# Layer norm and projection over eight pieces, Ln and Exp in place of square root and reciprocal, skip terms begun in the convolution, and the stored weights waited for later

## The reference, cut to what matters

```
xz = x @ W_in.T;  xc, z = split(xz);  xc = silu(conv3x3(xc) + conv_b)
x1, x2 = row order of xc, column order of xc;  x3, x4 = the same, flipped
for k in 0..3:                      # y_k has 256 channels and 4096 steps
    h = exp(dt*A)*h + (dt*u)*B;  y_k = sum_n h*C + u*D_k
y  = y_0 + y_2 flipped + (y_1 + y_3 flipped), back in row order
mu = mean(y, channels);  var = mean((y-mu)**2, channels)
y  = (y-mu) * rsqrt(var + 1e-5) * ln_w + ln_b
out = x + (y * silu(z)) @ W_out.T
t = out + attention(layer_norm(out));  result = t + spectral(layer_norm(t))
```

## Time and profile before

| what | value |
|---|---|
| median of 3 runs | 6822.46 us |
| the profiled execution, its time | 6814.78 us |
| its span (first to last instruction) | 6813.0 us |
| busy over the span | PE 86%, DVE 71%, ACT 51%, POOL 40% |
| convolution of image 0, PE's loop | 64 to 186 us |
| scans of image 0 | 186 to 1808.6 us |
| norm and projection of image 0 | 1809.3 to 1917.3 us |
| scans of image 1 begin | 2068.0 us |
| norm and projection of image 1 end | 3800.1 us |

### The profile page before, as it was taken

The page is one execution under the profiler, slowest core; times in us unless marked ns, Lnnn a source line. Parts: engine busy times, 40 slices in busy tenths (PEclk is TensorE's granted clock), DMA queues, the critical chain, the costliest instruction groups (busy, mean ns, idle before and its releaser), DMA issues. The chain is left out here.

```text
span 6813.0 us, 130427 instructions
## 1 busy us (share of the span) xinstructions
PE 5854.0 (86%) x41691; PEld 5166.6 (76%) x41691; DVE 4832.0 (71%) x6902; ACT 3505.3 (51%) x7656; POOL 2748.9 (40%) x2143
## 2 busy tenths in 40 slices
PE   7789888988777898898987553899999989999998
PEld 5688788888656787888876342788888878888887
DVE  2799999999727999999997564456555555655555
ACT  2799999999636999999996221111111111111110
POOL 0588888888505888888886000000000000000000
PEclk8899999999888999999998886899999989999999
DMA  2122222222211222222222113766766666666665
GB/s 65 70 86 88 88 82 87 87 88 84 81 61 69 83 87 88 83 93 81 89 87 73 48 33 103 166 150 151 153 136 142 149 154 150 154 152 142 144 149 146
DMA packets 554833, 719.10 MB, mean 106 GB/s; under 512 B 38198, under 2 KB 458902, under 8 KB 520470
## 3 DMA queue, kind: packets, MB, share of 16 engines
q1 hardware_dynamic: 553814, 705.17, 38.3%
q10 hardware_dynamic: 720, 10.49, 0.4%
HBM read 677.22 MB, written 38.31 MB: 105 GB/s over the span
## 5 line engine op out<-in xcount | busy, mean ns | idle before, releaser
L656 POOL TENSOR_TENSOR read<-state,c_wide 128x1024 f32<-128x1024 f32 x1024 | 2434.8, 2378 | 460.9 <-DVE state L718 455.7
L718 DVE TENSOR_TENSOR_SCAN state<-decay,carry,p_drive 128x512 f32<-128x512 f32 x1792 | 2145.9, 1259 | 9.9 <-PE p_drive L503 8.4
L610 ACT ACTIVATE decay<-step,a_neg 128x512 f32<-128x512 f32 x2048 | 1416.2, 714 | 230.1 <-DVE state L718 229.8
L1573 PE MATMUL p_y<-window,x_high 128*128 128x256 f32 x7936 | 1502.7, 287 | 0.0
L1636 ACT COPY term_blocks<-p_s 128x256 f32<-128x256 f32 x832 | 309.9, 372 | 2191.2 <-PE p_s L1573 2191.2
L1573 PEld LDWEIGHTS p_y<-window,x_high 128*128 128x128 f32 x7936 | 1250.7, 192 | 0.0
L503 PE MATMUL p_drive<-diag_b,xu_tok 128*128 128x128 f32 x8192 | 1107.0, 286 | 119.2 <-DVE state L718 115.3
L503 PEld LDWEIGHTS p_drive<-diag_b,xu_tok 128*128 128x128 f32 x8192 | 1013.1, 197 | 212.0 <-DVE state L718 150.3
L1573 PE MATMUL p_y<-window,x_low 128*128 128x256 f32 x3968 | 1136.8, 286 | 0.0
L514 PE MATMUL p_y<-ident,read 128*128 128x128 f32 x8192 | 1077.3, 275 | 3.8 <-POOL read L656 3.8
L514 PEld LDWEIGHTS p_y<-ident,read 128*128 128x128 f32 x8192 | 941.4, 143 | 4.7 <-POOL read L656 4.7
(11 more groups left out here) (246 smaller groups left out, 5883.8 us busy)
## 6 DMA issues: line engine op xcount, KB each, us to landing
c_wide<-c_scratch SPq DMA_DIRECT2D x256, 1024.0 KB, 4.7
window<-taps_scratch SPq DMA_DIRECT2D x448, 257.0 KB, 6.2
window<-taps_scratch SPq DMA_DIRECT2D x768, 129.0 KB, 4.5
window<-taps_scratch SPq DMA_DIRECT2D x192, 513.0 KB, 7.0
window<-taps_scratch SPq DMA_DIRECT2D x64, 385.0 KB, 6.0
gate_scratch<-gate_out SPq DMA_DIRECT2D x16, 512.0 KB, 3.1
gate_in<-gate_scratch SPq DMA_DIRECT2D x16, 512.0 KB, 4.9
mix_weights<-in_M_plus SPq DMA_DIRECT2D x32, 256.0 KB, 7.0
```

Of the source, the lines that this page charges most:

```text
L610: act.activation(decay[:, n % 2, t, :], step[:, c.parity, t, :], ACT.Exp, scale=m.a_neg[:, DT2 * c.k + t, n:n + 1]).then_inc(s["decay"], 1)
L656: pool.tensor_tensor(read[:, n % 4, :, :], state[:, n % 4, :, :], wide, ALU.mult).then_inc(s["read_out"], 1)
L718: dve.tensor_tensor_scan(flip(state[:, n % 4, t, :], c), flip(decay[:, n % 2, t, :], c), flip(p_drive[:, n % 2, t, :], c), 0.0 if c.start ...
L1573: last = pe.matmul(out, x[:, source, blk, :], view[:, :, at:at + P][:, :, ::-1], start=first and x is m.x_high and z == 0, stop=True, skip ...
```

## The change

Four things are edited.

- `constants` doesn't wait for the landing of the stored weights any more. The semaphore `w_stored` is kept to `convolution`, where SP waits for it just ahead of loading them.
- y is allocated for the whole first layer. In `convolution` POOL multiplies each group of 1024 tokens of `s1` by D_0+D_2 into y, when ACT has written it: 8 products of 128x1024 an image. `begin_y` keeps only the sums in column order; the one of tile 0 stands behind `step_bias` of both tiles, the one of tile 1 behind `finish_step`. `add_y` waits for them.
- `norm_and_project` is written out for eight pieces. In step k, PE does the mean of piece k, the variance of k-1 and the projection of k-3; ACT the square of k, and Ln, Exp and the affine step of k-1; DVE `centre` of k, `scale` of k-1 and the sum of k-3. `centred` and `work` exist four times, and the gate and x are loaded and the result stored in pairs of pieces (1024 tokens).
- 1/sqrt(var + eps) is Exp(-0.5 * Ln(var + eps)) on ACT, with one set of tables loaded at the block's start; the square root and DVE's reciprocal are gone.

The diff, cut to its core:

```
 constants
             sp.dma_start(m.w_conv_dram, w_conv...
-                         ).then_inc(w_out_dram, 16)
-            sp.wait_ge(w_out_dram, 16)
+                         ).then_inc(m.w_stored, 16)
 convolution
+            sp.wait_ge(m.w_stored, 16)
             sp.dma_start(w_conv...
         def _(pool):
+            with pool.Fori(0, NG) as g:
+                for t in range(DT2):
+                    pool.wait_ge(s["gated"], START + b * 17 + g * 4 + (4 + t))
+                    piece = ds(g * 1024, 1024)
+                    pool.tensor_tensor(m.y[:, t, piece], m.s1[:, t, piece],
+                                       m.d_skip[:, 8 + t:9 + t].broadcast_to([P, 1024]), ALU.mult)
 scans, vector
-            def begin_y():
-                for t in range(DT2):
-                    dve.tensor_scalar(m.y[:, t, :], m.s1[:, t, :], m.d_skip[:, 8 + t:9 + t], None, ...
-                dve.wait_ge(s["y_begun"], START + b * 4 + 2)
-                for t in range(DT2): ...
+            def begin_y(t):
+                y = m.y[:, t, :].rearrange("p (h w) -> p w h", w=W)
+                dve.scalar_tensor_tensor(y, m.s2[:, t, :].rearrange("p (w h) -> p w h", h=H), ...
                 if c.first:
-                    begin_y()
                     step_bias(c, 0)
                     step_bias(c, 1)
+                    begin_y(0)
                     finish_step(c)
+                    begin_y(1)
                     keep_x(c, 0)
 norm_and_project
+    RING = 4
-            with sp.Fori(0, N2) as j:
...
+            load(0)
+            load(1)
+            for pair in range(N2):
+                sp.wait_ge(s["added"], START + n0 + (2 * pair + 2))
+                sp.dma_start(tokens(m.t_dram, pair), t_out[:, pair % 2, :, :]).then_inc(...)
+                if pair + 2 < N2:
+                    load(pair + 2)
 tensor
+            for k in range(NCH + 3):
+                if k < NCH:
+                    mean(k)
+                if 0 <= k - 1 < NCH:
+                    variance(k - 1)
+                if 0 <= k - 3 < NCH:
+                    project(k - 3)
 scalar
+            def deviation(c):
+                act.wait_ge(s["variance"], START + n0 + (c + 1))
+                if c >= 2:
+                    act.wait_ge(s["scaled"], START + n0 + (c - 1))
+                act.activation(inv[:, c % 2, :], p_var[c % 2][:, :], ACT.Ln, bias=m.eps[:, 0:1])...
+                act.wait_ge(s["deviation"], START + n0 + (c + 1))
+                act.activation(inv[:, c % 2, :], inv[:, c % 2, :], ACT.Exp, scale=-0.5)...
+            act.preload_act_table_set("natural_log_exp_and_others")
+            for k in range(NCH + 1):
+                if k < NCH:
+                    square(k)
+                if k:
+                    deviation(k - 1)
+                    affine(k - 1)
 vector
-                    dve.reciprocal(inv[:, par, :], inv[:, par, :]).then_inc(s["inverse"], 1)
...
+            for k in range(NCH + 3):
+                if k < NCH:
+                    centre(k)
+                if 0 <= k - 1 < NCH:
+                    scale(k - 1)
+                if 0 <= k - 3 < NCH:
+                    add(k - 3)
```

More of the change, by code:

```diff
@@ L798, in norm_and_project @@
         ps = lambda n, sh: ctx.enter_context(nc.psum_tensor(n, sh, fp32))
[L799 to L802, removed]
+        gate = sb("gate_in", [P, 2, DT2, 2 * L])
+        x_in = sb("x_in", [P, 2, 8, C])
+        centred = sb("centred", [P, RING, DT2, L])
+        work = sb("work", [P, RING, DT2, L])
         inv = sb("inv", [P, 2, L])
-        t_out = sb("t_out", [P, 2, 4, C])
@@ L827, in _, with mean @@
         @block.tensor
         def _(pe):
-            with pe.Fori(0, N2) as j:
-                n0 = b * NCH + j * 2
-                for par in range(2):
-                    pe.wait_ge(s["centred"], START + n0)
+            def mean(c):
+                if c >= 2:
+                    pe.wait_ge(s["centred"], START + n0 + (c - 1))
+                for t in range(DT2):
+                    last = pe.matmul(p_mean[c % 2][:, :], m.mean256[:, :], m.y[:, t, L * c:L * c + L],
+                                     start=t == 0, stop=t == DT2 - 1)
+                last.then_inc(s["mean"], 1)
@@ new lines, in variance, with project @@
+            def variance(c):
+                pe.wait_ge(s["squared"], START + n0 + (c + 1))
+                if c >= 2:
+                    pe.wait_ge(s["deviation"], START + n0 + (c - 1))
+                for t in range(DT2):
+                    last = pe.matmul(p_var[c % 2][:, :], m.mean256[:, :], work[:, c % RING, t, :],
+                                     start=t == 0, stop=t == DT2 - 1)
+                last.then_inc(s["variance"], 1)
+            def project(c):
+                pe.wait_ge(s["gated"], START + n0 + (c + 1))
+                if c >= 2:
+                    pe.wait_ge(s["added"], START + n0 + (c - 1))
+                for i in range(4):
@@ L833, in _ @@
                     for t in range(DT2):
-                        last = pe.matmul(p_mean[:, par, :], m.mean256[:, :], m.y[:, t, ds(j * 2 * L + par * L, L)],
+                        last = pe.matmul(p_out[c % 2][:, i, :], work[:, c % RING, t, i * P:i * P + P], m.w_o[:, t, :],
                                          start=t == 0, stop=t == DT2 - 1)
-                    last.then_inc(s["mean"], 1)
-                for par in range(2):
-                    pe.wait_ge(s["squared"], START + n0 + (par + 1))
-                    for t in range(DT2):
-                        last = pe.matmul(p_var[:, par, :], m.mean256[:, :], work[:, par, t, :],
-                                         start=t == 0, stop=t == DT2 - 1)
-                    last.then_inc(s["variance"], 1)
@@ L843, in _ @@
-                for par in range(2):
-                    pe.wait_ge(s["gated"], START + n0 + (par + 1))
-                    for i in range(4):
-                        for t in range(DT2):
-                            last = pe.matmul(p_out[:, par, i, :], work[:, par, t, i * P:i * P + P], m.w_o[:, t, :],
-                                             start=t == 0, stop=t == DT2 - 1)
-                    last.then_inc(s["product"], 1)
+                last.then_inc(s["product"], 1)
+            for k in range(NCH + 3):
[5 more added lines that the diff above has]
+                    project(k - 3)
@@ L851, in _, with square @@
         @block.scalar
         def _(act):
[L853 to L868 removed]
+            def square(c):
+                act.wait_ge(s["centred"], START + n0 + (c + 1))
+                if c >= RING:
+                    act.wait_ge(s["product"], START + n0 + (c - RING + 1))
+                act.activation(work[:, c % RING, :, :], centred[:, c % RING, :, :], ACT.Square).then_inc(s["squared"], 1)
@@ new lines, in affine @@
+            def affine(c):
+                act.wait_ge(s["scaled"], START + n0 + (c + 1))
+                for t in range(DT2):
+                    last = act.activation(work[:, c % RING, t, :], centred[:, c % RING, t, :], ACT.Identity,
+                                          bias=m.ln_b[:, t:t + 1], scale=m.ln_w[:, t:t + 1])
+                last.then_inc(s["affine"], 1)
+            act.preload_act_table_set("natural_log_exp_and_others")
[5 more added lines that the diff above has]
+                    affine(k - 1)
```

120 lines of the change are left out of this document (49 added, 71 removed).

## The result

The changed kernel takes 6709.19 us (median of 4 runs, 6704.23 to 6719.07) against 6819.57 us of before in the same rounds (4 runs, 6806.2 to 6832.06). The ratio is 0.984, with a 95% interval of 0.9817 to 0.9863. In the rounds of the last experiments it was 0.9825 (0.9809 to 0.9842). The profiled executions are 6814.78 and 6713.79 us, spans 6813.0 and 6712.1, 100.9 us apart; 99.1 were forecast.

The account below looks back on a forecast made before the run. PE bounds the convolution, a chain of waits the norm. 6814.8 - 97.0 (norms) + 1.4 (scan starts) - 3.5 (stored weights) = 6715.7 us, or 6723 against the median; range 6705 to 6750.

Parts of the forecast that it names:

- Bound by its chain: Norm before: no engine always busy in a 26.9 us round, so the chain of waits between engines bounds it.
- The period: Norm: time per piece is the longest of PE at high clock, PE at low clock and DVE-ACT ring; 5.7 us.
- The ring: Norm: DVE and ACT in turn, square, Ln, Exp, scale, sum, centre; 5.7 us with handovers, 6.0 at the upper end.
- The norm: Whole norm of an image: 59 us (57 to 63) instead of 108.0; -97.0 us for both images.
- the late gate: Norm: loads of pairs 2 and 3, issued only behind a pair's second sum, cost 0 to 2 us, held by the 59.
- The rival of the low clock: Norm: PE stays at the low clock, 88 us for 59, +58 for both images, total 6781; chance 0.07 with mixtures.
- The chosen branch: Start of the scans: POOL's step_times_u waits for DVE's second sum, first copy 0.7 us later, +1.4 for both images.
- the row of L896: Trace row before: a DVE instruction takes 1.93 us, not 1.23, beside POOL's product; read as two-SBUF-input operations excluding each other.
- rival 1: Start of the scans: DVE's second sum does not hold POOL; -7.4 us against the forecast, total 6716; chance 0.28.
- the rival of a slow spread operand: Convolution: POOL's products with the spread D_0+D_2 hold its end; at 25 us each 6889; chance 0.01 with the like.
- The stored weights: End of the constants: SP's wait for the store goes, -3.5 us once.
- The sum: Whole kernel: -97.0 + 1.4 - 3.5 = -99.1 us, 6715.7 against the profiled execution, 6723 against the median; chance 0.55.

Follow-up runs that it names:

- the last experiments: The last rounds of measurement, in which the changed kernel was run again beside the best version: 6712.82 us, ratio 0.9825 against the kernel before.
- the run with the input from PSUM: Changed kernel with its second column-order sum cut in 8 parts that add to a PSUM tile instead of y: 6712.14 us, one execution.
- the product of one input that held POOL: Changed kernel with its second column-order sum replaced by a product reading one SBUF tensor, same walk through y: 6716.81 us, one execution.

## Why the prediction was right, point by point

- **Bound by its chain.** Right. Shortening the chain alone (Ln and Exp, 27 us) and overlapping alone (pipeline, 31 us) each took that much from a stage in which no engine was busy for more than 61% (PE, 16.34 of 26.90 us).
- **The period.** Forecast 5.7, measured 5.31. The ring is the one named. Exp is 0.63 and not 0.69, Ln out of PSUM 0.67, and instructions in a row start some 0.1 us before the last has ended, so that no handover of 0.05 us has to be added within an engine. From start to start the ring is `scale` 1.14, sum 0.60, `centre` 1.24, square 0.97, Ln 0.70, Exp 0.66. PE at the high clock is 5.22 (forecast 5.6), as forecast a near tie.
- **The norm.** Forecast 59, measured 57.65 and 56.35, and part of that closeness is luck. Until the first `scale` ends it takes 10.8 us (forecast 11.1). The seven periods behind it take 37.6 us where 39.9 were forecast: 4.3 us too many in the forecast, since the real period is shorter and the first and last steps lack the sum or the `centre`, against 2.1 us that the late load cost and the forecast did not have. From the last `scale` on it takes 9.2 us, forecast 7.2 to 9.0; of the last two projections the first ran at the low clock. The spare 3.3 us of POOL were taken to cover the late gate. What they don't cover is that POOL's late product shuts out DVE's `scale`, which is on the ring. The forecast saw that hold and had 0.3 us in hand against it; it is 0.1 us even where no load is late (POOL ends at 1834.69, `scale` starts at 1834.79).
- **Clock.** The rival of the low clock is wrong: 0.90 for the whole stage, and 1.00 from 1810.4 to 1840. PE's waits of up to 8 us between its steps are gone there. The low clock is left at the two ends: 0.50 in the first 4 us, and 0.62 from 1855.0 to 1861.5, after PE has waited 5.17 us. A wait doesn't always bring it: in the run with the input from PSUM the last projection of image 1 takes 2.05 us after 3.0 us of waiting.
- **Table loads.** The loads of a round went and one is left, as forecast. It isn't the change of functions that does it: straight code has one load with the square root too.
- **Start of the scans.** The chosen branch is right: POOL waits for the second sum (10.92 us), and the first copy is 0.41 us later, forecast 0.7. Moving 22 us of DVE's work won nothing, as the forecast said from the row of L896. The rule from "SBUF — State Buffer" in the Trainium skill ("Who interferes with whom"), which the working named, holds in this direction as well. The same section counts `tensor_scalar` among the one-input instructions that can take the shared ports, and says that others with at most one input in SBUF don't contend; the product of one input that held POOL (5.61 us), the sum with an input in PSUM and the reciprocal (2.36 and 2.34 us) agree with it. By time alone rival 1, POOL not held, would have looked better: its 6716 is nearer to 6709 than 6723 is. The 10.92 us in the trace decide against it.
- **POOL's products in the convolution** take 1.89 us and are hidden; the rival of a slow spread operand is wrong.
- **The stored weights.** 5.05 us came back, 3.5 forecast; 1.45 of it is that the work ahead of the wait was done earlier in this execution (DVE's last copy starts at 29.80 and not 31.25), which leaves 3.6 for the wait. In the other traces without the wait the first token load stands at 35.5 to 37.4, so that 1 us either way is spread.
- **The sum.** -99.1 forecast, -100.9 between the traces, -110 and -123 between medians. The forecast of 6723 was 14 us above the median. The mechanism is as forecast. That the two traces meet the size to 2 us is partly luck: the norms gave 3 us more than forecast and the start of the program 1.5 more, and 4.8 us in a part that nobody touched took that back. The sum was made against one execution of before whose unchanged last part was the shortest seen, and has no term for the spread of that part.

## What to carry to other kernels

In a stage where no engine is busy for most of the time, add up the ring of instructions that must come one after the other across engines, and compare it with each engine's own sum: the period is the longer of them. Writing such a stage out as a pipeline and taking slow steps off the ring are two gains that only partly overlap. Work moved beside other work is hidden only if the two may run together: DVE and POOL didn't when both read two tensors from SBUF, so put such work where the other engine sleeps, as the skip terms in the convolution. And when two such instructions meet, what counts is which of them is on the ring: the later one waits. Last, where a long stage that no edit touches varies by 20 us, compare times up to its start.

## What the runs showed of the hardware

- POOL is held for the whole of a DVE instruction with two inputs in SBUF (10.92 us for 2.34 of work), or with one input at 0.91 ns an element (5.61 us). It is not held where the second input is in PSUM (2.36 us), nor by a reciprocal (2.34). The hold works both ways: DVE's `scale` of 1.23 us took 3.30 when POOL's product had begun first, and POOL's product took 3.41 when `scale` had, 0.03 us ahead.
- A product on POOL of one tensor with one value a partition takes 1.89 us for 128x1024, where a product of two tensors takes 2.34 to 2.37.
- Adding in column order to y costs 8.9 us for 4096 elements in one instruction from SBUF, but 7.4 us in eight parts of 512 with the second input in PSUM, and 2.8 to 3.0 us for four parts of 256.
